# An attention step on TensorE: the side job placed behind the value products instead of ahead of them

## The reference

```python
q_mag, k_mag = softplus(x @ wq.T), softplus(x @ wk.T)     # per head of 16
q_embed = stack([q_mag * cos(qp), q_mag * sin(qp)])       # 32 per head
k_embed = stack([k_mag * cos(kp), k_mag * sin(kp)])
attn = softmax(q_embed @ k_embed.T / 4)                   # 1024 x 1024 per head
x = layernorm(x + (attn @ v) @ wo.T)
# experts: softmax gates, top 2 of 8, 640 rows of capacity each, 256 -> 1024 -> 256, gelu
x = layernorm(x + weighted_sum_of_expert_outputs)
```

## Time and profile before

| What | us |
|---|---|
| median of three runs | 920.64 (920.51 to 920.93) |
| the profiled execution | 919.06 |
| its span, from the first to the last instruction | 917.3 |
| TensorE's products busy | 882.7 (96%) |
| ScalarE busy | 732.4 (80%) |
| VectorE busy | 636.8 (69%) |
| GpSimd busy | 483.1 (53%) |

### The profile page before, as it was taken

How to read it: one execution, slowest core, us unless ns; L and a number is a source line. 1 busy time by engine, 2 the same in 40 slices (tenths; PEclk the granted TensorE clock), 3 DMA queues, 4 the chain that set the end, 5 groups by cost and what they waited for, 6 DMA issues and landing times. The chain is left out here.

```text
span 917.3 us, 20054 instructions
## 1 busy us (share of the span) xinstructions
PE 882.7 (96%) x7653; PEld 500.6 (55%) x7653; DVE 636.8 (69%) x1184; ACT 732.4 (80%) x895; POOL 483.1 (53%) x408
## 2 busy tenths in 40 slices
PE   8999999999999999999999999999499999999995
PEld 5434344334344433433443433334499999998994
DVE  5787547557986655798565676538557877888787
ACT  6788978898897899889789889898265787778874
POOL 3488345245565734747474444532413556666565
PEclk9999999999999999999999999999789999999998
DMA  5734466543535345253433425531261745534411
GB/s 179 170 131 157 143 215 222 194 173 116 201 129 188 115 127 220 91 198 134 158 126 128 162 99 196 180 101 52 89 200 41 253 135 179 173 114 133 157 60 66
DMA packets 62507, 135.45 MB, mean 148 GB/s; under 512 B 10558, under 2 KB 31398, under 8 KB 62272
## 3 DMA queue, kind: packets, MB, share of 16 engines
q1 hardware_dynamic: 41936, 72.88, 24.6%
q0 software_dynamic: 20464, 61.18, 19.0%
HBM read 69.20 MB, written 62.35 MB: 143 GB/s over the span
## 5 line engine op out<-in xcount | busy, mean ns | idle before, releaser
L815 ACT ACTIVATE prob<-spsum 128x1024 f32<-128x1024 f32 x512 | 492.8, 1022 | 81.3 <-PE spsum L1037 77.0
L1061 PE MATMUL opsum<-prob,val 128*17 128x512 f32 x2048 | 270.2, 597 | 4.4 <-ACT prob L815 1.9
L1037 PEld LDWEIGHTS spsum<-stacks 32*128 32x128 f32 x1536 | 73.3, 183 | 115.4 <-ACT prob L815 67.9
L1037 PE MATMUL spsum<-stacks 32*128 32x512 f32 x1536 | 134.9, 426 | 0.8 <-ACT prob L815 0.6
L1037 PEld LDWEIGHTS spsum<-area_q 32*128 32x128 f32 x1536 | 73.0, 183 | 112.4 <-ACT prob L815 57.6
L1037 PE MATMUL spsum<-area_q 32*128 32x512 f32 x1536 | 132.4, 425 | 1.0 <-ACT prob L815 0.9
L1455 DVE RECIPROCAL oden<-oden 128x256 f32<-128x256 f32 x62 | 108.7, 1753 | 2.1
L610 POOL TENSOR_TENSOR area_s<-emb,area_s 128x1024 fp32r<-128x1024 f32 x28 | 66.6, 2380 | 47.6 <-DVE area_s L1262 44.2
L696 POOL TENSOR_TENSOR onorm<-oraw,oden 128x512 f32<-128x512 f32 x31 | 42.1, 1359 | 93.2 <-DVE oden L1455 93.1
L1061 PEld LDWEIGHTS opsum<-prob,val 128*17 128x17 f32 x2048 | 39.4, 95 | 85.4 <-ACT prob L815 45.8
L608 POOL TENSOR_TENSOR square<-raw 128x512 bf16<-128x512 f32 x28 | 52.0, 1857 | 56.4 <-DVE raw L1235 56.3
(11 more groups left out here) (263 smaller groups left out, 1401.5 us busy)
## 6 DMA issues: line engine op xcount, KB each, us to landing
split_scratch<-area_s POOLq DMA_DIRECT2D x56, 512.0 KB, 4.1
area_k<-in_w SPq DMA_DIRECT2D x16, 1024.0 KB
area_q<-split_scratch SPq DMA_DIRECT2D x28, 512.0 KB
stacks<-split_scratch SPq DMA_DIRECT2D x24, 512.0 KB
rows<-dispatched SPq DMA_DIRECT2D x7, 662.5 KB
aT<-onorm SPq DMA_DIRECT2D x124, 32.0 KB
staged<-in_xT SPq DMA_DIRECT2D x7, 512.0 KB, 4.3
dispatched<-last_rows POOLq DMA_DIRECT2D x2, 1722.5 KB, 12.8
```

The costliest lines, as they stand in the source:

```text
L815: act.activation(prob[u % NPB][:], spsum[u % NSB][:].rearrange("p a n -> p (a n)"), ACT.Exp, scale=HD ** -0.5).then_inc(s_exp, 1)
L1037: ins = pe.matmul(spsum[u % NSB][:, j % 2, :], kst[par][rows, a, P * kt:P * (kt + 1)], qst[par][rows, b, cols], start=i == 0, stop=i == 2 ...
L1061: ins = pe.matmul(opsum[32 * j:32 * j + HD + 1, :], val[b % 2][:, kt, h0 + j, :], prob[(2 * s + j // 2) % NPB][:, HALF * (j % 2):HALF * (j ...
```

## The change

In each attention step TensorE's jobs stand behind the preceding step's value products. They used to stand between the scores and these products. Nothing else differs; the parts of a tile's job that `opened` starts early move with the jobs.

```diff
                     scores(s, shifted)
+                    if s > s0 or s and not shifted:
+                        values(s - 1)
                     if s in opened:
                         tile_part(opened[s], 0)
                     for job in jobs_at(s):
                         run(job)
-                    if s > s0 or s and not shifted:
-                        values(s - 1)
```

## The result

The kernel with the change takes 927.61 us (median of 4 runs, 926.55 to 929.55), beside 920.58 (920.20 to 920.93) before: a ratio of 1.0075, 95% interval 1.006 to 1.0091, so 7.0 us more (5.5 to 8.4). That is slower, as forecast, inside the range (921.0 to 929.5), and 2.4 us above the predicted 925.2. The profiled execution took 926.55, span 924.8, at the same mean granted clock as before, 0.988.

What follows compares the result with a forecast made beforehand. The prediction took TensorE as the bound, neck and neck with ScalarE in attention steps without a job. Terms 1.0 + 0.5 + 1.3 + 2.0 + 1.0 - 1.1 - 0.1 + 0 gave +4.6, so 925.2 us, range 921.0 to 929.5.

Steps and rivals of the forecast that it cites:

- likeliest case: The whole sum, +4.6 us for the kernel, chance 0.60, own range 922.9 to 928.
- Term 1: At the 102 job steps, values wait for their exponentials: +1.0 us, bounds 0 and 4.1.
- Term 2: Values wait for VectorE's accumulator copy: +0.5 us over steps 41, 49, 113 and 177, +1.3 at step 17.
- Term 3: At steps 88 and 152 VectorE's unbroken chain makes its accumulator copy later: +0.98 us twice, +2.0.
- Term 4: At the end of attention, step 249's job delays VectorE's gapless work up to the last outputs: +1.0 us.
- The gain at 79, 143 and 207: At these steps the tile job's wait for its bank goes: -0.38 us three times, -1.1.
- The gain at 56, 120 and 184: At these steps a norms job covers the 0.13 us wait for the accumulator copy: -0.1 us, to -0.4.
- Term 5: Hand-overs between TensorE groups of different tile shape in job steps cost the same in either order: 0.
- The prediction's last sign: Scores starting behind a job under 0.1 us less or more than values did would make the prediction fail there first.
- hand-over rival: Either untiled jobs' hand-overs save time (918.1 us, chance 0.10) or tile jobs lose warm ones (928.3, 0.13).
- The rival of the absorbed lateness: VectorE's lateness vanishes in stretches GpSimd sets: +1.1 us, 921.7; chance 0.17, counted together with no effect.

Runs made afterwards that it cites:

- middle: Kernel before, jobs behind values only at steps 18 to 245 but for 82 to 87 and 146 to 151: 922.11 us beside 920.45.
- chain only: Kernel before, jobs behind values only at steps 82 to 87 and 146 to 151: 921.68 us beside 920.45.
- start only: Kernel before, jobs behind values only at steps 1 to 17: 922.10 us beside 920.22.
- end only: Kernel before, jobs behind values only from step 246 on: 921.29 us beside 920.45.
- all-but-chain: Kernel before, jobs behind values everywhere but at steps 82 to 87 and 146 to 151: 924.81 us beside 920.45.
- norms alone: Kernel before, job behind values only at steps 56, 120 and 184: 920.22 us beside 920.40.

## Why the prediction was right, and where it was off

The mechanism is as predicted: whatever values wait for now stands ahead of the job instead of beneath it, and VectorE gets each job's bank one group of values later. The size was 4.6 for 7.0 (5.5 to 8.4), and the steps of the sum are off in both directions. That they partly cancel is luck: a gain that never came (-1.1), a missed step (0.3) and ScalarE's lateness (0.9 or more) stand against terms 1 to 3, which came out some 1.3 smaller together. The likeliest case's own range, 922.9 to 928, does not follow from the bounds either; these reach 929.0 (4.1 for term 1, 0.7 and 1.8 for term 2).

*Term 1 (+1.0).* The wait is right, its price half. Summed over the job steps that don't open a block, the values' idle time behind scores is 1.0 us by the distance of starts. But from scores to scores these steps are only 0.5 us longer together than before, as the hand-overs around them are up to 0.01 shorter each. That the middle, with most of these steps, holds only 2.0 excludes a much larger even price.

*Term 2 (+0.5 and +1.3).* At steps 41, 49, 113 and 177 values lose 0.13 to 0.14 each: right. At 17 they lose 0.78 in the changed kernel and 0.99 in the kernel with the start alone, under the predicted 1.3. VectorE's copy came 0.90 later, more than forecast, but TensorE's scores ahead of it had come 0.97 later (step 9, and a stall ahead of step 16 that is not the order's), and a wait counts from TensorE's arrival. So it stayed just under the lower bound of 0.84. Missed: step 9, 0.30. I had taken the copy there to have time to spare. VectorE stood idle for 1.00 ahead of it before (copy at 49.13); after the change it read step 5's job 1.01 later, had no idle time left, and the copy began at 49.49.

*Term 3 (+2.0).* 0.84 and 0.83 at two steps, 1.7 in all, shown by the twelve steps alone, which make the same two jumps, and by the others, which don't. At step 216 nothing came, as forecast. The 0.98 was too much since the chain begins at a norms job, and one of these starts 0.41 behind the last value product, where a projection's starts 0.52 behind it (below).

*Term 4 (+1.0).* 0.89, shown by the end alone.

*The gain at 79, 143 and 207 (-1.1).* This failed, and it is the largest error in the sum. The step was "VectorE was busy elsewhere, so the copy stays". VectorE was busy, but with a chain that itself begins at the tile job of step 75, and that moved as well. The first row is from the kernel before, the second from the changed one:

```profile
207.19 0.17 DVE L1303 TENSOR_TENSOR rt<-misc,xlog 128x8 f32<-128x8 f32 x1 [0.71 <-PE misc L879]
...
209.90 0.17 DVE L1303 TENSOR_TENSOR rt<-misc,xlog 128x8 f32<-128x8 f32 x1 [0.68 <-PE misc L879]
```

From there VectorE has no idle time to the copy in either kernel, and reaches it after 10.30 us before and 10.31 after. In between, its read of step 77's bank went from 213.64 to 216.35, by 2.71, and the copy at its end from 217.49 to 220.21, by 2.72, while the scores around shifted by 1.85. Bank and copy moved together, and the wait stayed. It is the reasoning of term 3, which I had applied 10 steps further on and not here. Without this gain the sum is +5.7. The place is shown by the two traces; no run moves these jobs alone.

*The gain at 56, 120 and 184 (-0.1).* The 0.13 is there at each. Behind it ScalarE's late exponentials grew: before, at step 185 and at step 121,

```profile
478.67 3.81 ACT L815 ACTIVATE prob<-spsum 128x1024 f32<-128x1024 f32 x4 [0.81 <-PE spsum L1037]
...
322.44 3.81 ACT L815 ACTIVATE prob<-spsum 128x1024 f32<-128x1024 f32 x4 [1.06 <-PE spsum L1037]
...
323.51 0.96 PE L1037 MATMUL spsum<-stacks 32*128 32x512 f32 x10 [0.24 <-ACT prob L815]
```

and after, at step 121:

```profile
325.64 3.82 ACT L815 ACTIVATE prob<-spsum 128x1024 f32<-128x1024 f32 x4 [1.50 <-PE spsum L1037]
...
326.72 0.97 PE L1037 MATMUL spsum<-stacks 32*128 32x512 f32 x10 [0.83 <-ACT prob L815]
```

TensorE's wait is 0.83 for 0.24. In the changed kernel this is worth 0.60 behind step 122 and 0.74 behind 186; but 0.45 shows one step later with the old order there (chain only, start only, end only), so it is 0.9 to 1.3 that belongs to the change. At step 186 the norms job behind values brings it about, as it shows with these jobs alone moved. At 122 it does not do so by itself: in that run nothing is added there, and what else is needed stays open.

*Term 5 (0).* Right, and now measured. From the last instruction of one group to the first of the next, us:

| pair | before | pair | after |
|---|---|---|---|
| scores to job | 0.32 | scores to values | 0.32 |
| `qk` job to values | 0.33 | values to `qk` job | 0.52 |
| `v` job to values | 0.21 | values to `v` job | 0.52 |
| tile job to values | 0.20 | values to tile job | 0.41 |
| values to scores | 0.52 | `qk`, `v`, tile job to scores | 0.32, 0.21, 0.32 |

The prediction's last sign looked at one pair alone: scores start 0.12 later behind a tile job than values did (0.32 for 0.20), over its 0.1 and at 31 jobs. The next pair gives this back (values to tile job 0.41, values to scores 0.52). For a tile job the three sum to 1.045 before (0.320 + 0.203 + 0.522) and 1.042 after (0.316 + 0.410 + 0.316). The tile job's weights are loaded ahead behind values, too (627.73 for a job that starts at 628.15). So neither hand-over rival came: the order costs nothing there. By the rule of the Trainium skill, TensorEngine Tiling (Array Packing), Key Properties, that changing the mode drains the array, the count of changes is the same in both orders. The trace agrees so far that the three hand-overs of a step with a `qk`, `v` or tile job sum to the same in both orders, within 0.02 us; a drain by itself it does not show.

*The rival of the absorbed lateness* fell: VectorE's chain took 12.14 for 12.15 us, and GpSimd's operation moved with it, by 2.78.

What the profiled execution holds: the scores of step 249 are 5.7 us later, and the end adds 0.9, so the last outputs (639.88 and 646.51) are 6.6 later. Of this, 0.6 ahead of step 16 and 0.9 ahead of 247 come and go without the order, and so may 0.45 at step 187. That leaves 4.7 to 5.1 for the order in this one execution; its span is 7.5 longer and the median time 7.0 (5.5 to 8.4). So about 2 us of the median's 7.0 have no place here, and what of them is the order's can't be said from one profile of each.

## What to carry to other kernels

When a result that another engine reads comes later, follow that engine's work back, in order, to where it last stood idle. If that idle time was ended by something that moves, all behind it moves, and a wait on it doesn't go away, whoever is named as its releaser. Do this for each wait that the sum counts, the gains first. And a filler job is worth most right where a hand-over between engines is exposed: behind the accumulator's copy it hides a wait, behind the values it hides none of theirs.

## What the runs showed of the hardware

ScalarE begins some exponentials 0.4 to 1.2 us after their scores are there, by the modelled end of these, while 0.04 is usual. Numbers 216, 242 and 344 are among them in every kernel here, also with 24 instructions more ahead of them, and 370 or 372. Others, such as 464, 466 and 508 in the kernel before, come and go. No record of the profile fills the gap, and its cause is open.

Two stalls come and go between kernels whose instructions there are the same. One is ahead of the scores of step 16: 0.4 to 0.6 us in the full change, all-but-chain, start only and norms alone, 0.2 or less in chain only, end only and middle. The other is 0.8 to 0.9 ahead of those of 247, behind a late exponential: in the full change, chain only and start only, and 0.2 or less in all-but-chain, end only and middle. So up to 1.5 us between two single profiles of this kernel can have no cause in the edit; the shift step by step tells which places to leave out.
